# Attention value products in four groups per pair: units 6 and 7 joined to unit 8, behind the next pair's first score unit

## The chip, the cores and the metric

The kernel runs on one core of a Trainium2 chip. The metric is the device time of one launch in microseconds; of several runs the median counts. TensorE (PE in the rows) multiplies, ScalarE (ACT) takes exponentials and copies, VectorE (DVE) takes maxima and other elementwise work, GpSimd (POOL) does small elementwise work, SyncE (SP) issues most of the transfers.

## The reference, cut to what matters

The block is a half-weighted attention-and-experts layer, a sparse attention with selected keys, and the first layer once more with the same weights:

```
x = x + 0.5 * ffn_ref(layernorm(x), ...)
x = x + attn_ref(layernorm(x), ...)
x = x + 0.5 * ffn_ref(layernorm(x), ...)
```

The change lies in the attention inside `ffn_ref` (2 batches of 1024 tokens, 16 heads of width 8, causal):

```
scores = jnp.einsum('bhqd,bhkd->bhqk', q, k) / jnp.sqrt(jnp.float32(hd))
causal = jnp.tril(jnp.ones((s, s), bool))
scores = jnp.where(causal, scores, jnp.finfo(scores.dtype).min)
attn = jax.nn.softmax(scores, axis=-1)
o = jnp.einsum('bhqk,bhkd->bhqd', attn, v)
```

## The kernel before

The program is `pe_ffn`, `pe_sel`, `pe_ffn` on TensorE and the like on the others: two passes over the layer (c = 0 and 1) with the sparse attention between them. In each pass the heads go in 16 pairs (2 batches x 16 heads / 2), so there are 32 pairs in the whole program; the two heads of a pair lie side by side in the array.

For each pair three things are computed. The first pass over the scores (`PASS1`, `pe_pass1`, line 758, with a causal mask added at line 763) serves only to find each row's maximum, which VectorE takes (`dve_max`, lines 1431 and 1441). The second pass (`PASS2`, `pe_scores`, line 789) computes the scores transposed, with the maximum already subtracted, because rows with the maximum (the "maxrows") are loaded into the query tile by two transfers (line 485). ScalarE takes the exponential (line 1185) into one of six buffers `PT`. The value products (`pe_values`, line 811) multiply these by the values and sum into PSUM bank 6. Both passes are cut into 9 units (0 to 8) of 4 blocks of 128 x 128 for both heads. Units 1, 2, 4, 6 and 8 hold blocks on the diagonal; GpSimd cuts those to a triangle (`pool_cut`, line 699) after the exponential and before the value product: one cut or two.

`pe_step` works on three pairs at once and sets TensorE's order by hand. It begins at unit 5 (`HALFWAY`) of pair it and ends at unit 4 of pair it+1; at each unit TensorE does the score unit of the pair, then a first-pass unit of pair it+2 (`pe_next`), then, at some units, a value group. The value groups of a pair are `GROUPS = [(0, 1), (2, 3), (4, 5), (6, 7), (8,)]`; group 0 is done behind unit 4, group 1 behind unit 5, group 2 behind unit 7, group 3 behind unit 8, and group 4 behind unit 0 of the next pair. `pe_outputs` (line 821) turns the summed result behind unit 2 of the next pair. The last two pairs of a pass have no `pe_next`, and for the last one `pe_values` of groups 3 and 4 follow each other.

The waits that tie these together:

- A score unit waits for the maximum of the first-pass unit two places before it, whose PSUM pair it takes over, and unit 0 waits for both maxrow transfers as well (`maxrow_loaded`, line 779). `pe_next` waits for the exponential of the score unit one place before it.
- A value group waits for the last exponential in it, or, if its last unit is on the diagonal, for the cuts up to it (`cut_done`, line 805). Group 3 ends in unit 7, so it waits for exponential 7 and for cut 6; group 4 waits for cut 8.
- The maxrows of the next pair are turned by TensorE behind unit 6 (`pe_maxrows`, line 772), copied by ScalarE (line 1194), and sent by SyncE (line 485, two transfers).
- ScalarE's exponentials of the next pair wait for the value groups that free their buffer: unit 0 for group 1, unit 1 for group 2, and units 3 and 4 for group 3. Behind exponential 1 ScalarE waits for all groups of the pair and copies bank 6 away (line 1208), then goes on with exponential 2.
- SyncE loads the rows of pair it+4 when all groups of pair it are done (line 465).

In the names of the rows, `twin` is PSUM, `arena` holds the exponentials, maxima and values, `ffn` the query and key tiles.

Of the kernel before, what the change touches and what calls it, by code (L numbers as in the profile page):

```python
# [143 lines left out]
PASS2 = [[(0, 0)], [(1, 0)], [(0, 1)], [(1, 1), (1, 6)], [(1, 2), (1, 7)], [(0, 2), (0, 5)], [(0, 3), (0, 6)], [(1, 3), (1, 4)],  # L144
         [(0, 4), (1, 5)]]
UNITS = len(PASS1)
GROUPS = [(0, 1), (2, 3), (4, 5), (6, 7), (8,)]
GROUP_OF = [g for u in range(UNITS) for g, us in enumerate(GROUPS) if u in us]
EARLY = 4
HALFWAY = 5  # L150
# [10 lines left out]
def places(u):  # L161

    at, out = 0, []
    for g, kc in PASS2[u]:
        p = first_block(g, kc)
        out.append((g, kc, p, at))
        at += 4 - p
    assert at == 4
    return out
# [65 lines left out]
def build(nc, ins, const_ap, rot_ap, mask_ap, out):  # L235
# [10 lines left out]
    with ExitStack() as ctx:  # L246
# [207 lines left out]

        EXP0, PV0, ATT0, GELU0, Y0, ACC0, MAX0, OTURN0, OT0 = S_RING, len(GROUPS), 2, 4, 2, 2, S_RING, 1, 1
        block = ctx.enter_context(nc.Block())
# [4 lines left out]
        def sp_rows(sp, c, it, buf):  # L461

            g = PAIRS * c
            if not isinstance(it, int) or c:
                sp.wait_ge(pv_done, PV0 + len(GROUPS) * (g + it - RING + 1))
            pair = slice(it, it + 1) if isinstance(it, int) else bass.ds(it, 1)
# [300 lines left out]
        def pe_maxrows(pe, c, it):  # L767

            n = PAIRS * c + it
            pe.wait_ge(att_done, ATT0 + n - 1)  # L770
            pe.wait_ge(mb_ready, n + 1)
            pe.transpose(bank[7][:, :].bitcast(BF16)[:, 0:P], MB, ident_b[:, :]).then_inc(mt_done, 1)

        def pe_scores(pe, c, it, buf, u, left):

            n = PAIRS * c + it
            m = UNITS * it + u
            if u == 0:
                pe.wait_ge(maxrow_loaded, 32 * n + 32)
            if left >= 2:  # L780
                pe.wait_ge(max_done, MAX0 + TOTAL * c + m + UNITS + EARLY - 1)
            else:
                pe.wait_ge(max_done, MAX0 + TOTAL * c + min(m + UNITS + EARLY - 1, TOTAL))
                pe.wait_ge(exp_done, EXP0 + TOTAL * c + m - S_RING + 1)
            slot = 2 * u % S_RING
            for j, (g, kc, p, at) in enumerate(places(u)):
                for s in range(2):
                    r = slice(TILE * s, TILE * (s + 1))
                    x = pe.matmul(bank[2 * slot + s][:, at * P:(at + 4 - p) * P], KB[buf][r, kc * P:(kc + 1) * P],  # L789
                                  QB[buf][r, (4 * g + p) * P:(4 * g + 4) * P], start=(j == 0), stop=True, skip_group_check=True)  # L790
            x.then_inc(st_done, 1)

        def pe_next(pe, c, it, buf, m, u, visit):

            pe.wait_ge(exp_done, EXP0 + TOTAL * c + m)
            pe_pass1(pe, c, it, buf, u, visit, (2 * ((u + HALFWAY) % UNITS) + 1) % S_RING)

        def pe_values(pe, c, it, buf, group):

            n = PAIRS * c + it  # L800
            if group == 0:
                pe.wait_ge(ot_ready, OT0 + n)
            if GROUPS[group][-1] not in CUT:
                pe.wait_ge(exp_done, EXP0 + UNITS * n + GROUPS[group][-1] + 1)
            pe.wait_ge(cut_done, len(CUT) * n + len([u for u in CUT if u <= GROUPS[group][-1]]))
            for u in GROUPS[group]:
                for g, kc, p, at in places(u):
                    for s in range(2):
                        r = (2 * s + g) * STRIP
                        v = (s * TB + kc) * VW  # L810
                        m = pe.matmul(bank[6][r:r + STRIP, p * P:], VS[buf][:, v:v + STRIP],  # L811
                                      PT[(UNITS * buf + u) % PT_RING][:, s, at * P:(at + 4 - p) * P], start=(kc == 0), stop=True,
                                      skip_group_check=True)
            m.then_inc(pv_done, 1)

        def pe_outputs(pe, c, it):

            pe.wait_ge(att_done, ATT0 + PAIRS * c + it)
            pe.wait_ge(ot_ready, OT0 + PAIRS * c + it + 1)
            for t in range(4):  # L820
                m = pe.transpose(bank[7][:, t * P:(t + 1) * P], OT[:, t * P:(t + 1) * P], ident)
            m.then_inc(o_turned, 1)

        def pe_step(pe, c, b, it, buf, left, visit):
            two, one = (buf + 2) % RING, (buf + 1) % RING
            for u in range(HALFWAY, UNITS):
                pe_scores(pe, c, it, buf, u, left)
                if left >= 2:
                    pe_next(pe, c, it + 2, two, UNITS * it + u, u - HALFWAY, visit + (buf + 2) // RING)
                if u == HALFWAY:  # L830
                    pe_values(pe, c, it, buf, 1)
                if u == HALFWAY + 1 and left >= 1:
                    pe_maxrows(pe, c, it + 1)
                if u == HALFWAY + 2:
                    pe_values(pe, c, it, buf, 2)
                if u == HALFWAY + 3:
                    pe_values(pe, c, it, buf, 3)
            if left == 0:
                pe_values(pe, c, it, buf, 4)
                pe_outputs(pe, c, it)  # L840
                return
            for u in range(HALFWAY):
                pe_scores(pe, c, it + 1, one, u, left)
                if left >= 2:
                    pe_next(pe, c, it + 2, two, UNITS * (it + 1) + u, u + EARLY, visit + (buf + 2) // RING)
                if u == 0:
                    pe_values(pe, c, it, buf, 4)
                if u == 2:
                    pe_outputs(pe, c, it)
                if u == 4:  # L850
                    pe_values(pe, c, it + 1, one, 0)

        def pe_ffn(pe, c):
# [29 lines left out]
            for u in range(HALFWAY):  # L883
                pe_scores(pe, c, 0, 0, u, PAIRS)
                pe_next(pe, c, 1, 1, u, u + EARLY, 0)
            pe_values(pe, c, 0, 0, 0)
            run_steps(pe, pe_step, c)

            pe.wait_ge(att_done, ATT0 + PAIRS * (c + 1))
# [1043 lines left out]
```

## Time and profile before

| | us |
|---|---|
| median of 3 runs | 1869.47 (1865.15, 1869.47, 1881.36) |
| the profiled execution | 1864.45 |
| its span, first to last instruction | 1862.3 |

| engine | busy us | share of the span |
|---|---|---|
| TensorE matmul | 1476.3 | 79% |
| VectorE | 1244.6 | 67% |
| ScalarE | 996.6 | 54% |
| GpSimd | 445.8 | 24% |

The pairs run from about 78 to 304 us (first pass over the layer) and from about 1384 to 1609 us (second). Shares of the whole span say little about them: the experts and the sparse attention take the rest. A timeline of one pair, read row by row, shows what each engine waits for; a row with a bracket gives the idle time ahead of an instruction and what ended it. Rows of the same line that follow each other are merged, so the start of the next line's row tells when an engine went on.

### The profile page before, as it was taken

The numbers are of one execution on the slowest core, as the hardware profiler recorded it, in microseconds if no ns is written. First come the engines' busy times: TensorE is split into PE (matmuls) and PEld (weight loads), VectorE is DVE, ScalarE is ACT, GpSimd is POOL, SyncE is SP. The second block draws the span as 40 slices with busy tenths as digits, with TensorE's granted clock in tenths as the row PEclk, the third lists the DMA queues.
The fourth block names the chain that finished last, engine by engine and source line by source line (L and its number), as shares of the span: only waits on it lengthen the run. The fifth ranks groups of instructions, "written<-read, shape, count | busy, mean of one in ns | idle before, by whom it ended". The sixth has DMA issues, their size and how long they took to land.

```text
span 1862.3 us, 31801 instructions
## 1 busy us (share of the span) xinstructions
PE 1476.3 (79%) x10514; PEld 948.3 (51%) x10580; DVE 1244.6 (67%) x2571; ACT 996.6 (54%) x1800; POOL 445.8 (24%) x751
## 2 busy tenths in 40 slices
PE   3699997899958365888877888778469999779995
PEld 2355554577744122455545555556335455467774
DVE  3688885577785657675666676644367788567777
ACT  2266665588846342434444445334226666568884
POOL 4122222000011500434344344440412232200000
PEclk8699998699987556988778899788769999879998
DMA  5111110121102234111121111120221110011110
GB/s 156 67 49 44 43 30 2 58 68 68 57 23 76 67 82 95 52 26 55 27 72 54 34 51 53 35 62 17 91 83 48 46 45 30 2 58 68 68 57 23
DMA packets 63685, 99.68 MB, mean 54 GB/s; under 512 B 20011, under 2 KB 43507, under 8 KB 61494
## 3 DMA queue, kind: packets, MB, share of 16 engines
q1 hardware_dynamic: 53910, 80.42, 14.0%
q0 software_dynamic: 8192, 16.79, 3.5%
q8 instruction: 72, 1.18, 0.3%
q10 hardware_dynamic: 1456, 0.84, 0.2%
q14 instruction: 55, 0.45, 0.1%
HBM read 73.42 MB, written 10.69 MB: 45 GB/s over the span
## 4 chain that ended last, share of the span: by engine, by line
PE 51%; DVE 11%; ACT 9%; issue 9%; another core or an unknown queue 6%; DMA 5%; DVEq 4%; SPq 2%; ACTq 1%; POOL 0%; POOLq 0%
PE twin L964 9%; PE twin L954 6%; PE twin L811 5%; PE twin L789 5%; PE twin L758 4%; PE twin L1118 4%; DMA ffn<-arena 3%; DVEq L1750 3%; ACT arena L1185 3%; ACT experts L1260 2%; PE twin L763 2%; PE twin L1146 1%; PE twin L1134 1%; PE twin L1162 1%
## 5 line engine op out<-in xcount | busy, mean ns | idle before, releaser
L1185 ACT ACTIVATE arena<-twin 128x1024 f32<-128x1024 f32 x288 | 293.9, 1024 | 176.5 <-PE twin L789 176.3
L736 POOL DMA_INDIRECT arena<-kv_rows,IDX x256 | 249.1, 973 | 447.4 <-PE twin L1165 308.6
L1441 DVE TENSOR_REDUCE arena<-twin 128x8 f32<-128x1024 f32 (+1 forms) x160 | 195.4, 1225 | 81.3 <-PE twin L758 41.9
L1490 DVE TENSOR_TENSOR experts<-arena,experts 128x512 fp32r<-128x512 f32 x256 | 171.6, 690 | 71.2 <-ACT experts L1260 71.2
L1258 ACT ACTIVATE arena<-twin,bias 128x512 f32<-128x512 f32 x256 | 185.8, 726 | 45.8 <-PE twin L954 45.8
L954 PE MATMUL twin<-experts,experts 128*128 128x512 f32 x768 | 196.7, 403 | 7.5 <-ACT experts L1260 5.5
L758 PE MATMUL twin<-ffn,ffn 64*128 64x128 f32 (+3 forms) x1152 | 154.1, 350 | 48.1 <-DMA arena<-arena 27.0
L1431 DVE TENSOR_REDUCE arena<-twin 128x2 f32<-128x1024 f32 x128 | 153.2, 1222 | 52.5 <-PE twin L758 49.0
L1260 ACT ACTIVATE experts<-twin,bias 128x512 fp32r<-128x512 f32 x256 | 187.1, 731 | 0.0
L964 PE MATMUL twin<-experts,experts 128*128 128x512 f32 x768 | 182.2, 389 | 0.0
L1814 DVE TENSOR_TENSOR HN<-twin,RT 96x512 f32<-96x512 f32 x128 | 87.3, 683 | 135.1 <-remote 85.1
L699 POOL TENSOR_SCALAR_AFFINE_SELECT arena<-arena 128x256 f32<-128x256 f32 x256 | 100.1, 409 | 316.2 <-ACT arena L1185 316.2
L954 PEld LDWEIGHTS twin<-experts,experts 128*128 128x128 f32 x768 | 143.8, 192 | 54.7 <-ACT experts L1260 22.2
L789 PE MATMUL twin<-ffn,ffn 64*128 64x128 f32 (+3 forms) x960 | 145.9, 368 | 25.0 <-DMA ffn<-arena 21.0
L811 PE MATMUL twin<-arena 128*32 128x128 f32 (+3 forms) x1920 | 159.7, 433 | 2.6 <-POOL arena L699 1.6
L964 PEld LDWEIGHTS twin<-experts,experts 128*128 128x128 f32 x768 | 144.2, 188 | 30.4
L633 POOL TENSOR_TENSOR rstd<-vareps,neghalf 128x8 f32<-128x8 f32 x14 | 23.5, 1676 | 549.0 <-DVE vareps L1420 549.0
L758 PEld LDWEIGHTS twin<-ffn,ffn 64*128 64x128 f32 x1152 | 96.6, 202 | 78.6 <-ACT arena L1185 30.9
L789 PEld LDWEIGHTS twin<-ffn,ffn 64*128 64x128 f32 x960 | 76.6, 188 | 115.4 <-issue 75.1
L1392 ACT ACTIVATE ATT<-twin,col 128x256 f32<-128x256 f32 x128 | 60.7, 474 | 133.7 <-DVE col L1823 103.1
L1385 ACT ACTIVATE ATT<-twin 128x384 f32<-128x384 f32 (+1 forms) x128 | 55.8, 436 | 122.1 <-remote 112.7
L1118 PE MATMUL twin<-XN,arena 128*128 128x512 bf16 x374 | 113.2, 447 | 8.5 <-issue 7.4
(253 smaller groups left out, 2291.2 us busy)
## 6 DMA issues: line engine op xcount, KB each, us to landing
arena<-wt_rows SPq DMA_DIRECT2D x16, 1024.0 KB, 4.9
arena<-in_L_ffn_w SPq DMA_DIRECT2D x32, 256.0 KB, 5.2
ffn<-q_rows SPq DMA_DIRECT2D x64, 128.0 KB
ffn<-k_rows SPq DMA_DIRECT2D x64, 128.0 KB
XT<-idx_rows SPq DMA_DIRECT2D x16, 512.0 KB
q_rows<-ffn SPq DMA_DIRECT2D x8, 512.0 KB, 4.9
k_rows<-ffn SPq DMA_DIRECT2D x4, 1024.0 KB, 9.2
arena<-kv_rows,IDX POOLq DMA_INDIRECT x256
```

Of the source, the lines that this page charges most:

```text
L736: pool.indirect_dma_start(G[d % GR][:, g, :], None, kv_rows, bass.IndirectOffsetOnAxis(ap=IDX[:, q, k * GB + g:k * GB + g + 1], axis=0))\
L758: m = pe.matmul(bank[2 * slot + s][:, at * P:(at + blocks) * P], QB[buf][r, q * P:(q + 1) * P], KB[buf][r, k0 * P:(k0 + blocks) * P], star ...
L789: x = pe.matmul(bank[2 * slot + s][:, at * P:(at + 4 - p) * P], KB[buf][r, kc * P:(kc + 1) * P], QB[buf][r, (4 * g + p) * P:(4 * g + 4) * ...
L811: m = pe.matmul(bank[6][r:r + STRIP, p * P:], VS[buf][:, v:v + STRIP], PT[(UNITS * buf + u) % PT_RING][:, s, at * P:(at + 4 - p) * P], sta ...
L954: m = pe.matmul(bank[f][:, :], W1R[buf][w][:, f * P:(f + 1) * P], XR[x][:, tb * BANK:(tb + 1) * BANK], start=((w, x) == pairs[0]), stop=(( ...
L964: m = pe.matmul(bank[4 + k][:, :], W2R[buf][w][:, f, :], H1R[k][x][:, f, :], start=(f == 0 and (w, x) == pairs[0]), stop=(f == FC - 1 and ...
L1118: m = pe.matmul(o[:, :], TAB[part][:, 4 * b + c, :], OH[OH_AT[x][c] % OHR][:, :], start=(c == 0 and part == 0), stop=(c == n - 1 and part ...
L1185: act.activation(PT[(UNITS * buf + u) % PT_RING].rearrange("p s n -> p (s n)"), twin[2 * u % S_RING][:, :], ACT.Exp, scale=float(HD) ** -0 ...
L1258: act.activation(H1[tb % 2][:, f, :], bank[f][:, :], ACT.Gelu_apprx_tanh, bias=bias1[buf][:, f:f + 1])
L1260: act.activation(H1R[tb % 2][0][:, f, :], bank[f][:, :], ACT.Gelu_apprx_tanh, bias=bias1[buf][:, f:f + 1]).then_inc(gelu_done, 1)
L1441: dve.tensor_reduce(to, scores.rearrange("p (s t k) -> p s t k", s=2, t=to.shape[2]), AX_X, ALU.max).then_inc(max_done, 1)
L1490: dve.tensor_tensor(H1R[tb % 2][1][:, f, :], H1[tb % 2][:, f, :], H1R[tb % 2][0][:, f, :].bitcast(F32), ALU.subtract)\
```

## The change

Units 6, 7 and 8 become one group, number 3, done where group 4 was done: behind score unit 0 and the first-pass unit of the next pair. Nothing stands any more behind unit 8. For the last pair of a pass the group follows the last score unit. The counts in the waits follow from `GROUPS`.

```diff
-GROUPS = [(0, 1), (2, 3), (4, 5), (6, 7), (8,)]
+GROUPS = [(0, 1), (2, 3), (4, 5), (6, 7, 8)]
@@
                 if u == HALFWAY + 2:
                     pe_values(pe, c, it, buf, 2)
-                if u == HALFWAY + 3:
-                    pe_values(pe, c, it, buf, 3)
             if left == 0:
-                pe_values(pe, c, it, buf, 4)
+                pe_values(pe, c, it, buf, 3)
                 pe_outputs(pe, c, it)
                 return
             for u in range(HALFWAY):
@@
                 if u == 0:
-                    pe_values(pe, c, it, buf, 4)
+                    pe_values(pe, c, it, buf, 3)
```

On TensorE, at the boundary between two pairs, the rows stand as follows before (program order; L789 is a score unit, L758 a first-pass unit, L811 a value group, L779 the wait for the maxrows; the first two rows are unit 8, the rows behind L779 are units 0 and 1 of the next pair):

```order
L789 MATMUL twin<-ffn_65,ffn_69 128x256 x4
L795 REGISTER_ALU
L758 MATMUL twin<-ffn_71,ffn_67 128x512 x2
L805 REGISTER_ALU
L811 MATMUL twin<-arena 32x384 x2
L811 MATMUL twin<-arena 32x128 x2
L811 MATMUL twin<-arena 32x256 x4
L779 ISA
L781 ISA
L789 MATMUL twin<-ffn_66,ffn_70 128x512 x2
```

Here the value products of units 6 and 7 (the three rows of L811) stand between the first-pass unit and the wait for the maxrows. The difference at this place and at the next value group, which was that of unit 8 alone:

```order
 L758 MATMUL twin<-ffn_71,ffn_67 128x512 x2
-L805 REGISTER_ALU
-L811 MATMUL twin<-arena 32x384 x2
-L811 MATMUL twin<-arena 32x128 x2
-L811 MATMUL twin<-arena 32x256 x4
 L779 ISA
 L781 ISA
```

```order
 L758 MATMUL twin<-ffn_71,ffn_67 128x384 x2
 L805 REGISTER_ALU
-L811 MATMUL twin<-arena 32x256 x4
+L811 MATMUL twin<-arena 32x384 x2
+L811 MATMUL twin<-arena 32x128 x2
+L811 MATMUL twin<-arena 32x256 x8
 L781 REGISTER_ALU
 L789 MATMUL twin<-ffn_66,ffn_70 128x512 x2
```

The eight matmuls of units 6 and 7 left the first place, and the second has twelve where it had four; the last row, score unit 1 of the next pair, now has all twelve in front of it. Each matmul of the order is two in the trace (float32), so 16 left and 24 stand where 8 stood.

## Rows read from the trace of the kernel before

**Rows 1.** Chain of waits from 186 us: start, length, what held it
```profile
186.68 0.27 ACT arena L1194
186.95 0.02 issue
186.96 0.82 SPq L485
187.79 0.04 issue
187.83 2.20 DMA ffn<-arena
190.03 0.12 issue
190.15 0.50 PE twin L789 x2
190.65 0.29 PE twin L758 x4
190.94 0.58 PE twin L811 x8
```

**Rows 2.** Timeline of one boundary, all engines: start, length, engine, line, [idle, releaser]
```profile
159.22 0.40 PE L758 MATMUL twin<-ffn,ffn 64*128 64x512 f32 x2
159.50 1.02 ACT L1185 ACTIVATE arena<-twin 128x1024 f32<-128x1024 f32 x1 [1.06 <-PE twin L789]
159.55 1.08 PE L811 MATMUL twin<-arena 128*32 128x384 f32 x16
160.66 0.77 POOL L699 TENSOR_SCALAR_AFFINE_SELECT arena<-arena 128x256 f32<-128x256 f32 x2 [2.36 <-ACT arena L1185]
160.70 0.50 PE L789 MATMUL twin<-ffn,ffn 64*128 64x512 f32 x2
161.03 0.45 PE L758 MATMUL twin<-ffn,ffn 64*128 64x128 f32 x4
161.48 0.64 PE L811 MATMUL twin<-arena 128*32 128x256 f32 x8
162.05 0.50 PE L789 MATMUL twin<-ffn,ffn 64*128 64x512 f32 x2
162.67 1.02 ACT L1185 ACTIVATE arena<-twin 128x1024 f32<-128x1024 f32 x1 [0.41 <-PE twin L789]
163.75 0.50 PE L758 MATMUL twin<-ffn,ffn 64*128 64x256 f32 x4 [0.44 <-ACT arena L1185]
```

**Rows 3.** The same timeline, TensorE, value groups 0, 1 and 2 and what follows each
```profile
153.03 1.06 PE L811 MATMUL twin<-arena 128*32 128x512 f32 x8
154.02 0.50 PE L789 MATMUL twin<-ffn,ffn 64*128 64x384 f32 x4
...
154.74 1.07 PE L811 MATMUL twin<-arena 128*32 128x512 f32 x12
155.74 0.50 PE L789 MATMUL twin<-ffn,ffn 64*128 64x384 f32 x4
...
157.86 1.08 PE L811 MATMUL twin<-arena 128*32 128x384 f32 x16
158.88 0.51 PE L789 MATMUL twin<-ffn,ffn 64*128 64x256 f32 x4
```

**Rows 4.** Timeline, boundary 14 of the first pass and the last pair's end
```profile
291.50 0.49 PE L789 MATMUL twin<-ffn,ffn 64*128 64x512 f32 x2 [0.45 <-DMA ffn<-arena]
...
294.82 0.63 PE L821 MATMUL twin<-const,arena 128*128 128x128 f32 x4 [1.47 <-ACT arena L1208]
...
302.88 0.64 PE L811 MATMUL twin<-arena 128*32 128x256 f32 x8 [0.65 <-POOL arena L699]
```

**Rows 5.** Stretches of the pairs: busy us (instructions) by engine, granted clock, DMA
```profile
90.00:207.00 117.00, 109.05 (x1072) 59.35 (x1080) 93.16 (x112) 76.67 (x89) 33.93 (x104) 1.00 0.14 45
280.00:310.00 30.00, 24.12 (x248) 14.76 (x250) 9.70 (x23) 19.82 (x25) 7.36 (x21) 1.00 0.01 3
```

**Rows 6.** Timeline, ScalarE's copy of bank 6 in two pairs in a row
```profile
148.91 0.59 ACT L1208 ACTIVATE arena<-twin 128x512 f32<-128x512 f32 x1
...
163.59 0.59 ACT L1208 ACTIVATE arena<-twin 128x512 f32<-128x512 f32 x1
```

## The prediction

> **What bounds the kernel now.** First I read the pairs' granted clock and busy shares, since a mean over the program hides them: from 90 to 207 us TensorE is busy 109.05 of 117 us, VectorE 93.16, ScalarE 76.67, at a granted clock of 1.00 [rows 5]. So TensorE's order sets the pair's length, and at the upper of its two clock levels. That alone does not say that every matmul lies on the path. The chain of waits says where it does not: it leaves TensorE at the copy of the maxrows on ScalarE (186.68), goes through SyncE's issue (186.96) and the transfer (187.83, 2.20 us), and comes back to TensorE with score unit 0 of the next pair at 190.15 [rows 1]. In that stretch of 3.2 us TensorE does score unit 8, a first-pass unit and value groups, and none of it is in the chain.
>
> Next I read one boundary row by row [rows 2]. Behind unit 8 the first-pass unit starts at 159.22, the value group of units 6 and 7 at 159.55, score unit 0 of the next pair at 160.70, its first-pass unit at 161.03, the value group of unit 8 at 161.48, score unit 1 at 162.05. On the other engines exponential 8 runs from 159.50 to 160.52 and its two cuts on GpSimd from 160.66 to 161.43. Score unit 1 releases exponential 1 (162.67, one step of 1.02), and that releases the first-pass unit at 163.75, ahead of which TensorE is idle for 0.44 us.
>
> **The change part by part.** *What leaves the old place.* Sixteen matmuls of the trace, the group at 159.55. Groups of the same size with nothing to wait for behind them take, from their start to the start of what follows, 154.02 - 153.03 = 0.99, 155.74 - 154.74 = 1.00 and 158.88 - 157.86 = 1.02 us [rows 3]. This one takes 160.70 - 159.55 = 1.15 [rows 2], so score unit 0 waited 0.13 us more than the group explains, and the chain shows for what: the maxrow transfers. When the group is gone, TensorE is free at about 159.6, but score unit 0 still cannot start before the transfers have landed, about 3.2 us after their issue [rows 1], an issue that the change does not touch. So it stays at 160.70, and I credit the removal with nothing; TensorE idles about 1.1 us there.
>
> There is a second lid on any gain. Suppose the transfers were early: unit 0 could start at about 159.6, but its first-pass unit waits for exponential 8 (160.52), and the joined group waits for the cuts of unit 8, over at 161.43. Score unit 8, which leads to these, lies ahead of both places and does not move. So the joined group starts at 161.48 as before, whatever unit 0 does.
>
> *What comes to the new place.* The group at 161.48 takes 162.05 - 161.48 = 0.57 us for the columns of one unit spread over both halves of the output strips; the full groups have twice the columns per strip and take 1.00 on average. Twice as many columns thus cost 0.43 us more, and the joined group has three times those of unit 8: 0.57 + 2 x 0.43 = 1.43 us. The order of its units in the strips differs a little from those of rows 3, and no group of three is in the trace. Bounds: at best 0.57 + 2 x (0.99 - 0.57) = 1.41, with one entry and one exit for the group; at worst the sum of both groups as they are, 1.02 + 0.57 = 1.59. That is a growth of 0.84 to 1.02, and I take 0.86, since the step between group sizes is measured and the entry is saved.
>
> *Where the delay goes.* Score unit 1 starts 0.86 later, and everything that follows hangs on it. Queued behind the group on TensorE are score unit 1, first-pass unit 5, score unit 2. Exponential 1 waits for score unit 1 and slips by as much, then the first-pass unit at 163.75. The 0.44 us of idle there are no reserve: they are the time of exponential 1, counted from score unit 1, and remain. ScalarE's copy of bank 6 stands behind exponential 1 (which in rows 2 ends at 163.69, 1.64 us behind the end of the group), so its wait for all groups adds nothing more. Exponentials 3 and 4, which need the old group 3, come behind that copy already. SyncE's row loads start 0.86 later, but so do their readers, more than a pair ahead. VectorE gets its maxima later and has slack: 23.84 us of 117 [rows 5]. From unit 2 on to the turning of the maxrows the chain stays on TensorE's queue, so the next transfers, and with them the next unit 0, slip by the full amount.
>
> *The low clock.* The idle at the boundary grows from about 0.13 to 1.1 us. In this trace a boundary with idles of 0.45 and 1.47 us [rows 4] lies in a stretch with a granted clock of 1.00 [rows 5], which is the 2.4 GHz level. So I keep the clock. The Trainium skill, "TensorE: Matmul & The Clock Gate", section "A second HAM failure mode: psum-queue depth-cycling", says that short idles between groups of matmuls can make the clock swing between its two levels; by it this change would cost more than the moved matmuls, and it is a rival below. The rows with more idle speak against it here.
>
> *How many times.* The 14 boundaries of each pass that still have first-pass work are as in rows 2. Boundary 14 waits for the transfer too, with 0.45 us idle [rows 4], so its group is covered as well. Behind the last pair's unit 8 the old group of units 6 and 7 ran while GpSimd cut unit 8; after it TensorE waited another 0.65 us until 302.88 for those cuts [rows 4]. Now all three units start at 302.88: again 0.86. That is 16 per pass, 32 in all.
>
> **Sum.** 32 x 0.86 = 27.5 us, bounds 32 x 0.84 = 26.9 and 32 x 1.02 = 32.6. Against the profiled execution's 1864.45 that is 1892; the median of the three runs is 5 us above it, which makes 1897. I say 1895, or 1.4% slower. The copies of bank 6 of two pairs in a row start 163.59 - 148.91 = 14.68 us apart [rows 6]; that should grow to about 15.55 us.
>
> **The rivals.**
>
> *The delay is absorbed (no change).* This is the case on the other side. It needs a wait on TensorE between score unit 1 and the turning of the maxrows that score unit 1 does not itself cause, such as VectorE freeing a PSUM pair late. It decides in favour of no change if such a wait is 0.86 us or more in each pair; half of it gives 1864 + 14 = 1878 to 1883. The busy 109.05 of 117 leave 8 us over 8 pairs, 1.0 per pair, and 0.44 of that is exponential 1, so at most 0.5 could be there. With all of it absorbed the kernel would stay at 1869.
>
> *The saved switch counts (slightly faster).* If score unit 0 were not held by the transfers and the joined group not by the cuts, only one entry to a group would be saved: 1.02 + 0.57 - 1.43 = 0.16 us, 32 times, 5 us: 1864. Both holds would have to be misread.
>
> *The joined group is longer than its columns.* At 1.59 us or somewhat more, because units 6 and 7 follow each other in the same strips: 33 us or more, 1902.
>
> *The clock falls.* If one tenth of TensorE's work in the pairs ran at 1.2 GHz, that is at double length, a pair would grow by another 109.05 / 8 x 0.1 = 1.4 us, 32 times 44 us: about 1939.
>
> **How the numbers follow.** My forecast has 0.74; the longer group 0.09; the fallen clock 0.04; partly or fully absorbed 0.11; the saved switch 0.02. The range 1880 to 1910 takes in the forecast against either base, the longer group and half absorption, and leaves out the clock and full absorption. One per cent, about what a measurement of this kernel can tell from no change, is 18.7 us, so the limit lies at 1888: the forecast is beyond it save for a scatter like that of the runs (1865 to 1881). Slower 0.84, within 1% 0.14, faster 0.02.
>
> **What would show it.** In the profile after: score unit 0 (L789) still about 3.1 to 3.2 us behind the issue at L485, now with some 1.1 us of idle ahead of it, released by the transfer; the L811 group behind it with 24 matmuls, starting as the cuts of L699 end; score unit 1 about 1.43 us behind the group's start where it was 0.57; the copies at L1208 about 15.55 us apart; a granted clock of 1.00 from 90 to 280 us; nothing changed in the length of the experts and the sparse attention. I would be wrong if unit 0 and the group both started earlier against L1194, if the group took about 1.0 us, or if the copies stayed 14.7 us apart.

## The result, and the profile after

The changed kernel takes 1898.49 us (median of 4 runs, 1893.88 to 1904.39) where the kernel before takes 1867.31 (4 runs, 1861.28 to 1881.36). The ratio is 1.0159, with a 95% interval of 1.0125 to 1.0192: slower by about 30 us. The profiled execution has a span of 1891.7 us, 29.4 more than the span before.

Where those 29.4 us lie can be read from stretches of the two traces that end at the same event, ScalarE's copy of bank 6 in the first and in the last pair of each pass. Columns: stretch, its length, busy us (instructions) of TensorE, its weight loads, VectorE, ScalarE, GpSimd, then granted clock, share and GB/s of the transfers. The kernel before:

```profile
0.00:90.11 90.11, 46.37 (x264) 28.37 (x266) 44.57 (x94) 23.36 (x44) 26.18 (x53) 0.73 0.38 112
90.11:303.59 213.48, 196.94 (x1948) 106.57 (x1962) 158.37 (x195) 142.59 (x164) 62.48 (x190) 1.00 0.12 38
303.59:1395.40 1091.81, 825.64 (x5446) 540.51 (x5482) 695.96 (x1659) 515.58 (x1140) 287.88 (x314) 0.81 0.19 56
1395.40:1608.43 213.03, 197.12 (x1948) 106.61 (x1962) 158.24 (x195) 142.51 (x164) 62.49 (x190) 1.00 0.12 38
1608.43:1862.30 253.87, 210.19 (x908) 166.24 (x908) 187.45 (x430) 172.52 (x292) 6.72 (x4) 0.89 0.15 50
```

The changed kernel:

```profile
0.00:90.58 90.58, 47.16 (x266) 28.69 (x266) 44.58 (x94) 23.36 (x44) 26.18 (x53) 0.76 0.38 112
90.58:318.46 227.88, 195.30 (x1962) 107.46 (x1962) 158.35 (x195) 142.60 (x164) 62.48 (x190) 0.99 0.12 35
318.46:1412.04 1093.58, 836.19 (x5482) 540.72 (x5482) 694.93 (x1659) 515.01 (x1141) 287.51 (x314) 0.82 0.19 55
1412.04:1639.45 227.41, 195.03 (x1962) 107.48 (x1962) 158.24 (x195) 142.53 (x163) 62.47 (x190) 0.99 0.11 35
1639.45:1891.70 252.25, 208.55 (x908) 164.59 (x908) 187.47 (x430) 172.14 (x292) 6.72 (x4) 0.90 0.15 51
```

The two stretches of pairs grow by 14.40 and 14.38 us; the others change by +0.47, +1.77 and -1.62. TensorE's busy time in the pairs does not grow (196.94 to 195.30 us): the added time is idle. The two traces have 1948 and 1962 matmul records there, so the small fall is not read.

One boundary in the timeline of the changed kernel, which answers to [rows 2] (start, length, engine, line, idle ahead and its releaser):

```profile
177.14 1.62 SPq L485 DMA_DIRECT2D ffn<-arena  x2
...
178.80 0.39 PE L758 MATMUL twin<-ffn,ffn 64*128 64x512 f32 x2
179.08 1.02 ACT L1183 ACTIVATE arena<-twin 128x1024 f32<-128x1024 f32 x1 [1.06 <-PE twin L789]
...
180.23 0.77 POOL L699 TENSOR_SCALAR_AFFINE_SELECT arena<-arena 128x256 f32<-128x256 f32 x2 [2.37 <-ACT arena L1183]
...
180.33 0.50 PE L789 MATMUL twin<-ffn,ffn 64*128 64x512 f32 x2 [1.14 <-DMA ffn<-arena]
...
180.66 0.46 PE L758 MATMUL twin<-ffn,ffn 64*128 64x128 f32 x4
...
181.06 1.52 PE L811 MATMUL twin<-arena 128*32 128x384 f32 x24
...
182.51 0.49 PE L789 MATMUL twin<-ffn,ffn 64*128 64x512 f32 x2
```

Score unit 0 starts 3.19 us behind the issue at L485, as in [rows 1] (186.96 to 190.15), with 1.14 us of idle ahead of it that the transfer ends. The cuts of unit 8 are over at 181.00 and the joined group of 24 matmuls starts at 181.06. Score unit 1 follows 1.45 us behind the group's start; before it was 0.57. The chain of waits passes here, as in [rows 1], through the transfer and then the group:

```profile
161.28 0.27 ACT arena L1192
...
161.56 0.83 SPq L485
...
162.44 2.17 DMA ffn<-arena
...
164.72 0.50 PE twin L789 x2
...
165.51 1.49 PE twin L811 x20
```

The copies of bank 6 (now line 1206) start 15.58 us apart in the first seven intervals of the first pass, where they were 14.70. Two of them in a row:

```profile
168.46 0.59 ACT L1206 ACTIVATE arena<-twin 128x512 f32<-128x512 f32 x1
...
184.04 0.59 ACT L1206 ACTIVATE arena<-twin 128x512 f32<-128x512 f32 x1
```

The last interval, which belongs to the pair without first-pass work, grows from 9.51 to 11.62 us. That is more than 0.88, and the experiments below take it up.

### The profile page after: what moved, and what is told of

Read it like the earlier page. It is cut to its first block, busy times and chain, and to the rows that moved or that the text cites. A ratio compares the mean times of both kernels' runs of the same rounds, so it can differ in the third digit from the quotient of the medians.

```text
span 1891.7 us, 31827 instructions
## 1 busy us (share of the span) xinstructions
PE 1482.2 (78%) x10580; PEld 948.9 (50%) x10580; DVE 1243.6 (66%) x2571; ACT 995.6 (53%) x1800; POOL 445.4 (24%) x751
## 4 chain that ended last, share of the span: by engine, by line
PE 50%; DVE 12%; ACT 9%; issue 8%; another core or an unknown queue 7%; DMA 6%; DVEq 4%; SPq 3%; ACTq 1%; POOL 0%; POOLq 0%
PE twin L962 9%; PE twin L952 6%; PE twin L811 6%; PE twin L789 5%; PE twin L758 4%; DMA ffn<-arena 4%; PE twin L1116 3%; DVEq L1748 3%; ACT arena L1183 2%; PE twin L763 2%; ACT experts L1258 2%; PE twin L1144 1%; SPq L485 1%; DVE best L1789 1%
## 5 line engine op out<-in xcount | busy, mean ns | idle before, releaser
L758 PE MATMUL twin<-ffn,ffn 64*128 64x128 f32 (+3 forms) x1152 | 152.1, 346 | 54.5 <-DMA arena<-arena 26.5
L789 PE MATMUL twin<-ffn,ffn 64*128 64x128 f32 (+3 forms) x960 | 142.8, 361 | 54.8 <-DMA ffn<-arena 52.5
L811 PE MATMUL twin<-arena 128*32 128x128 f32 (+3 forms) x1920 | 155.6, 438 | 4.8 <-POOL arena L699 4.5
L789 PEld LDWEIGHTS twin<-ffn,ffn 64*128 64x128 f32 x960 | 76.6, 188 | 140.8 <-issue 80.2
L758 PEld LDWEIGHTS twin<-ffn,ffn 64*128 64x128 f32 x1152 | 98.5, 202 | 85.1 <-ACT arena L1183 39.6
L1116 PE MATMUL twin<-XN,arena 128*128 128x512 bf16 x408 | 129.8, 469 | 0.2 <-DVE HN L1812 0.2
```

What stands on the lines that cost most here:

```text
L758: m = pe.matmul(bank[2 * slot + s][:, at * P:(at + blocks) * P], QB[buf][r, q * P:(q + 1) * P], KB[buf][r, k0 * P:(k0 + blocks) * P], star ...
L1116: m = pe.matmul(o[:, :], TAB[part][:, 4 * b + c, :], OH[OH_AT[x][c] % OHR][:, :], start=(c == 0 and part == 0), stop=(c == n - 1 and part ...
```

## The experiments

The theory has three parts: the products of units 6 and 7 were free where they stood, because TensorE waits there for the maxrow transfers; they could not start the group earlier in the new place, because the transfers and, behind them, the cuts of unit 8 hold it; and score unit 1, hence exponential 1, hence the pair, pays for the group's length. Rivals: the wait of the joined group for the cuts makes the loss, or the transfer alone, or the clock. The table sums up the two kernels and the nine experiments. Each ratio compares a kernel with the kernel before in the same series of runs, whose median was 1867.31 us for the changed kernel, 1869.40 for e2 to e5 and 1865.59 for e1 and e6 to e8. "Pair" is the mean of the first seven intervals between copies of bank 6 in the first pass, "last" its last interval, "first copy" the start of the first.

| kernel | ratio to before (95%) | first copy | pair us | last us |
|---|---|---|---|---|
| before | 1 | 90.11 | 14.70 | 9.51 |
| changed | 1.0159 (1.0125 to 1.0192) | 90.58 | 15.58 | 11.62 |
| e2 without products 6 and 7 | 1.0014 (0.9989 to 1.0039) | 91.52 | 14.70 | 11.95 |
| e1 moved, not joined | 1.0136 (1.0095 to 1.0176) | 90.27 | 15.54 | 9.50 |
| e3 no transfer to wait for | 1.0073 (1.0047 to 1.0099) | 83.08 | 15.57 | 10.74 |
| e4 no cuts of unit 8 | 1.0117 (1.0073 to 1.0161) | 91.84 | 15.54 | 9.45 |
| e5 neither | 0.9952 (0.9932 to 0.9972) | 82.94 | 15.15 | 9.47 |
| e6 last pair split | 1.0153 (1.0112 to 1.0193) | 91.21 | 15.58 | 9.51 |
| e9 last pair's idle filled | one run | 90.95 | 15.57 | 10.36 |
| e7 unit 8 behind score unit 1 | 0.9951 (0.9927 to 0.9974) | 89.26 | 14.23 | 9.52 |
| e8 joined group behind score unit 1 | 1.0017 (0.9999 to 1.0036) | 88.27 | 14.81 | 10.57 |

### e2: were the products free in the old place?

```diff
             for u in GROUPS[group]:
+                if u in (6, 7):
+                    continue
                 for g, kc, p, at in places(u):
```

(on the changed kernel)

> The changed kernel with the value products of units 6 and 7 left out (so its attention sums lack them); the group behind the next pair's first score unit is unit 8 alone, as before the change. My theory: in the kernel before, these products ran while TensorE had to wait for the maxrow transfers anyway, so taking them out of it altogether gives nothing: 1862 to 1869 us, copies at L1206 14.6 to 14.7 us apart, score unit 0 still 3.1 to 3.2 us behind the issue at L485 with 1.0 to 1.2 us idle ahead of it. Rival (the products were on the path): 32 x 1.0 us less than before, about 1835 us, copies 13.7 us apart.

The ratio to the kernel before is 1.0014 (0.9989 to 1.0039), the pair 14.70 us, the same as before. Leaving out 16 matmuls of a pair buys nothing. TensorE's timeline shows the hole that they filled, released by the transfer, and the small group at 0.57 us as before:

```profile
176.89 0.49 PE L789 MATMUL twin<-ffn,ffn 64*128 64x512 f32 x2 [1.13 <-DMA ffn<-arena]
177.22 0.45 PE L758 MATMUL twin<-ffn,ffn 64*128 64x128 f32 x4
177.61 0.64 PE L813 MATMUL twin<-arena 128*32 128x256 f32 x8
178.18 0.50 PE L789 MATMUL twin<-ffn,ffn 64*128 64x512 f32 x2
```

The changed kernel differs from this one only by those products, in their new place, and costs 0.88 us a pair more. So the old place was free and the new one is not. The median, 1872.39 us, is 3 us over the upper end that I gave; the kernel before had 1869.4 beside it. The last interval is 11.95, 2.4 more than before (11.93 in the second pass). The rows say why:

```profile
295.00:301.00 6.00, 4.88 (x27) 2.47 (x28) 0.64 (x4) 3.83 (x5) 1.58 (x4) 0.50 0.00 0
...
306.62 0.64 PE L813 MATMUL twin<-arena 128*32 128x256 f32 x8 [2.11 <-POOL arena L699]
```

From 295 to 301 us, behind the boundary into the last pair, the granted clock was at its lower level, 0.50, and TensorE's work of that stretch took longer. Ahead of the very last group stand 2.11 us of idle, and that group ran at its usual 0.64 us. So the 2.4 us were lost ahead of that idle and not in it.

### e1: the move or the join?

```diff
-                if u == HALFWAY + 3:
-                    pe_values(pe, c, it, buf, 3)
             if left == 0:
+                pe_values(pe, c, it, buf, 3)
                 pe_values(pe, c, it, buf, 4)
@@
                 if u == 0:
+                    pe_values(pe, c, it, buf, 3)
                     pe_values(pe, c, it, buf, 4)
```

(on the kernel before)

> The kernel before with its five groups; only the place of group 3 (units 6 and 7) moves, to just ahead of group 4 (unit 8) behind the next pair's first score unit and first-pass unit. The last pair keeps the old order. My theory: score unit 1 slips by a whole group of 1.0 us in 30 pairs, pairs of 15.6 to 15.75 us, 1896 to 1901 us: the move alone makes the loss, and joining saves about 0.15 us per pair of it. Rival (the loss comes from the joined group's wait for the cuts of unit 8): units 6 and 7 need no such wait here, so pairs of 14.7 to 15.1 us and 1867 to 1880 us.

The ratio is 1.0136 (1892.08 us, below the 1896 to 1901 that I gave) and the pair 15.54 us. The rival falls: units 6 and 7 wait for no cut of unit 8 here, and the loss is still there. But my own number was off too. TensorE's timeline:

```profile
180.23 0.45 PE L758 MATMUL twin<-ffn,ffn 64*128 64x128 f32 x4
180.61 1.52 PE L811 MATMUL twin<-arena 128*32 128x384 f32 x24
182.06 0.50 PE L789 MATMUL twin<-ffn,ffn 64*128 64x512 f32 x2
```

The two separate groups take 182.06 - 180.61 = 1.45 us together, what the joined one takes too. In length, two groups that stand next to each other are no longer than one of the same columns; the join itself saves nothing, and the sum of the two lengths, 1.59, which I had as the upper bound, is not reached. The pair is 0.04 us shorter than in the changed kernel.

### e3, e4, e5: what holds the joined group?

e3 sends the maxrows to memory that nothing reads and drops the wait; e4 leaves unit 8 out of the cuts; e5 does both.

```diff
-                sp.dma_start(QB[buf][r:r + MAXROWS, :].bitcast(F32).rearrange("r (t q) -> r t q", q=P),
+                sp.dma_start(HNf[s * MAXROWS:(s + 1) * MAXROWS, 0:L].rearrange("r (t q) -> r t q", q=P),
@@
-            if u == 0:
-                pe.wait_ge(maxrow_loaded, 32 * n + 32)
@@
             pe.wait_ge(att_done, ATT0 + PAIRS * (c + 1))
+            pe.wait_ge(maxrow_loaded, 32 * PAIRS * (c + 1))
```

(e3; the last line makes TensorE wait for the transfers once, when all pairs of a pass are done)

```diff
-CUT = [u for u in range(UNITS) if diagonals(u)]
+CUT = [u for u in range(UNITS) if diagonals(u) and u != 8]
```

(e4)

> The changed kernel, but the maxrows are sent to memory nobody reads and score unit 0 does not wait for them (the maxima are not subtracted before the exponential). My theory of two lids: score unit 0 starts about 1.1 us earlier, its first-pass unit about 0.45 us earlier (behind exponential 8), but the joined group still starts when the cuts of unit 8 are over, so the time stays within 3 us of the changed kernel, about 1895 to 1900 us. Rival (the transfer alone holds the boundary): 28 x 1.1 us less, about 1868 us.

The pair is 15.57 us against 15.58: for the pairs the theory of two lids holds to 0.01 us. The timeline of e3 shows score unit 0 right behind the first-pass unit (171.51), the next first-pass unit waiting for exponential 8, and the group waiting for the cuts:

```profile
171.28 0.39 PE L758 MATMUL twin<-ffn,ffn 64*128 64x512 f32 x2
171.51 0.40 PE L787 MATMUL twin<-ffn,ffn 64*128 64x512 f32 x2
172.64 0.55 PE L758 MATMUL twin<-ffn,ffn 64*128 64x128 f32 x4 [0.73 <-ACT arena L1182]
173.54 1.52 PE L809 MATMUL twin<-arena 128*32 128x384 f32 x24 [0.34 <-POOL arena L699]
```

Score unit 0 is early and nothing comes of it. The total nevertheless fell, to a ratio of 1.0073 (1881.05 us), which is outside what I had written. The table says where: the first copy of the pass comes at 83.08 instead of 90.58, because the very first pair also stops waiting for its transfer. First the changed kernel, then e3:

```profile
69.00 0.80 PE L789 MATMUL twin<-ffn,ffn 64*128 64x512 f32 x2 [9.49 <-DMA ffn<-arena]
```

```profile
60.89 0.80 PE L787 MATMUL twin<-ffn,ffn 64*128 64x512 f32 x2 [1.25 <-DVE arena L1428]
```

The second pass has the same (9.78 us of idle against 1.25). The last interval is 10.74 instead of 11.62, and not through the missing wait: the idle ahead of the last group is 2.11 us in both kernels, but in e3 the granted clock fell only while the group ran, and it took 1.90 us instead of 2.79. That is 7.5 + 0.9 = 8.4 us a pass, 17 in all, about the 17.4 by which the medians differ (16 by the ratios). I had priced the boundaries and forgotten that the edit also takes the wait off the start.

> The changed kernel without the triangle cuts of unit 8 on GpSimd (its diagonal blocks stay uncut); the joined group waits for exponential 8 instead. My theory: the maxrow transfer still sets score unit 0 and with it the group's start, so the pairs stay at 15.5 to 15.6 us; only the last pair of each pass gains, 0.8 us by itself, up to 2 if its clock stays up: 1894 to 1898 us. Rival (the cuts alone hold the group): 28 x 0.45 or more, 1885 us or less.

The pair stays at 15.54, the last interval falls to 9.45, the median is 1893.8 us, just below what I gave: as the theory has it, the cuts alone hold nothing in the pairs. In the last pair the group then waits for exponential 8 alone. One thing was not foreseen: the interval before the last, with the boundary into the pair without first-pass work, is 15.95 us here against 14.86 in the changed kernel, and TensorE's timeline shows why:

```profile
303.56 0.50 PE L789 MATMUL twin<-ffn,ffn 64*128 64x512 f32 x2 [1.54 <-DMA ffn<-arena]
303.99 2.58 PE L811 MATMUL twin<-arena 128*32 128x384 f32 x24
```

The group takes 2.58 us instead of 1.52: in this execution the granted clock had fallen here (0.50 from 305 to 307 us), and in the second pass too (15.90 against 14.65).

> Both of the last two together: maxrows sent aside and unit 8 not cut. My theory: with both lids off the group starts behind the first-pass unit that waits for exponential 8, about 0.45 us earlier than in the changed kernel, 28 times, and the two ends of a pass gain too: pairs of about 15.1 us, 1880 to 1886 us. The joined group still costs its length behind exponential 8, so the time does not come back to 1867. Rival (any idle ahead of unit 0 is given back once nothing holds it): pairs of 14.5 us, 1866 us.

The pair is 15.15 us, 0.43 less than in the changed kernel, against 0.45 expected. With both lids off the group starts earlier, at 0.49 us behind its first-pass unit's start, which waits for exponential 8:

```profile
170.37 0.55 PE L758 MATMUL twin<-ffn,ffn 64*128 64x128 f32 x4 [0.73 <-ACT arena L1182]
170.86 1.52 PE L809 MATMUL twin<-arena 128*32 128x384 f32 x24
```

The rival's pair of 14.5 us is out. The median, 1860.31, is far below my 1880 to 1886, for the reason of e3 (7.6 us a pass at the start) and 2.15 us a pass in the last interval (0.9 because the group starts earlier, the rest because it runs at the upper clock). Those, the pairs (13 x 0.43) and boundary 14 (1.1) add up to 33 us; the ratios of the two kernels differ by 0.0207, 39 us, and the spans of the two profiled executions by 26.3 us, because in this one the part between the two passes' pairs took some 7 us longer. e5's profiled run was the slowest of its ten. The sum is thus right only to some 6 us either way, about the width of the intervals, and what the remainder is stays open.

### e6 and e9: why the last pair costs 2.1 us

The tail of the changed kernel, TensorE's timeline:

```profile
313.01 0.50 PE L789 MATMUL twin<-ffn,ffn 64*128 64x256 f32 x4
315.63 2.79 PE L811 MATMUL twin<-arena 128*32 128x384 f32 x24 [2.11 <-POOL arena L699]
```

Here the same 24 matmuls take 2.79 us instead of 1.52. In the stretches of that trace the granted clock is 1.00 until 313 and 0.50 from 316 to 319:

```profile
306.00:313.00 7.00, 5.54 (x62) 2.89 (x60) 0.64 (x4) 6.38 (x8) 1.61 (x5) 1.00 0.00 0
313.00:316.00 3.00, 0.89 (x12) 0.50 (x12) 0.00 (x0) 1.68 (x2) 1.51 (x4) 0.95 0.02 5
316.00:319.00 3.00, 2.42 (x24) 1.18 (x16) 0.00 (x0) 0.54 (x1) 0.00 (x0) 0.50 0.00 0
```

Before, the products of units 6 and 7 lay in this idle (the row of 302.88 in [rows 4] has 0.65 ahead of it). e6 gives them back their place in the last pair only:

```diff
+            if split:
+                pe.wait_ge(exp_done, EXP0 + UNITS * n + 8)
+                pe.wait_ge(cut_done, len(CUT) * n + 4)
...
-            pe.wait_ge(cut_done, len(CUT) * n + len([u for u in CUT if u <= GROUPS[group][-1]]))
+            if not split:
+                pe.wait_ge(cut_done, len(CUT) * n + len([u for u in CUT if u <= GROUPS[group][-1]]))
             for u in GROUPS[group]:
+                if split and u == 8:
+                    pe.wait_ge(cut_done, len(CUT) * n + 5)
```

> The changed kernel, but in the last pair of each pass the products of units 6 and 7 do not wait for the cuts of unit 8; those of unit 8 do. My theory: the profile after shows the last joined group at 2.79 us behind 2.11 us of idle, because the clock fell to its lower level in the idle; without that idle the group runs at the upper level again, and the last two copies at L1206 lie 9.5 us apart instead of 11.6: 4 us less than the changed kernel. Rival (only the order matters, not the clock): 0.9 us per pass, 1.8 in all.

The last interval is 9.51 us, as before the change. The total, 1.0153, can't tell 4 us from 2, the less so as in the second pass of the profiled execution the clock fell one boundary earlier (that interval is 16.12 us against 14.65 in the changed kernel). And e6 takes away the idle and the order together. e9 therefore keeps the wait and the order of the changed kernel and only fills the idle:

```diff
             if left == 0:
+                pe.wait_ge(exp_done, EXP0 + UNITS * (PAIRS * c + it) + 7)
+                for _ in range(8):
+                    pe.matmul(bank[0][:, :], ident_b[:, :], mask_qk[:, :, :].rearrange("p a q -> p (a q)"),
+                              start=True, stop=True, skip_group_check=True)
                 pe_values(pe, c, it, buf, 3)
```

> The changed kernel with eight idle-filling matmuls (a constant times a constant, result not read) in the last pair of each pass, between the last score unit and the joined group, while TensorE waits there for the cuts of unit 8. The wait itself stays. Clock theory: the fall to the lower level in this idle is what stretches the last group; filled, it runs at a granted clock of 1.00, takes 1.45 to 1.55 us, and the last two copies at L1206 lie 10.3 to 10.5 us apart (9.51 and 0.88) instead of 11.62. Rival (the group is long for another reason, such as its wait for the cuts or its 24 matmuls after a wait): still 2.7 to 2.8 us and 11.6.

```profile
313.28 0.50 PE L789 MATMUL twin<-ffn,ffn 64*128 64x256 f32 x4
313.72 1.90 PE L839 MATMUL twin<-mask_qk_b,ident_b 128*128 128x512 bf16 x8
315.90 1.52 PE L811 MATMUL twin<-arena 128*32 128x384 f32 x24 [0.28 <-POOL arena L699]
```

The group starts at the same distance from the score unit (315.90 - 313.28 = 2.62 us, in the changed kernel 315.63 - 313.01 = 2.62), takes 1.52 us at a granted clock of 1.00, and the last interval is 10.36 us in both passes, 0.85 over the kernel before. So of the 2.11 us, 0.85 are the group's length on the path and 1.26 are the lower clock. That the group ran at the lower clock is read from the changed kernel's own rows. That the idle brings the fall rests on less: e9 is one run, on a chip where the kernel before took 1748.04 us and this one 1772.48, and the changed kernel without filler was not run there. Only its trace is used; its pairs are 15.57 us, as on the first chip.

Nor does such an idle always cost the same. Four kernels have the 2.11 us of idle ahead of the last group, each in both passes. In the changed kernel the clock fell before the group (2.79 and 2.81 us), in e3 and e8 while it ran (1.90, 1.77, 1.73 and 1.68 us), and in e2 the group kept its 0.64 us. At the boundary into the last pair seven kernels have 1.40 to 1.56 us of idle ahead of score unit 0: there the clock fell in six of fourteen cases (both passes of e2 and e4, the second of e6 and e8) and held in eight (both passes of the changed kernel, e1 and e9, the first of e6 and e8). With 1.56 us it fell in two cases and held in one. So the length of one idle does not decide it, and what does stays open.

### e7 and e8: the group behind score unit 1

If exponential 1 pays for what stands ahead of score unit 1, a group should stand behind it. e7 does this with unit 8 of the kernel before, e8 with the joined group. The edit of e7:

```diff
                 pe_scores(pe, c, it + 1, one, u, left)
+                if u == 1:
+                    pe_values(pe, c, it, buf, 4)
                 if left >= 2:
                     pe_next(pe, c, it + 2, two, UNITS * (it + 1) + u, u + EARLY, visit + (buf + 2) // RING)
-                if u == 0:
-                    pe_values(pe, c, it, buf, 4)
```

(on the kernel before; e8 is the same edit on the changed kernel, with group 3)

> The kernel before with group 4 (unit 8) moved from ahead of score unit 1 of the next pair to just behind it. Score unit 1 then starts 0.57 us earlier; exponential 1 follows exponential 0 without a gap and ends 0.35 to 0.4 us earlier, and the group fills idle of TensorE. My theory: 0.35 to 0.4 us per pair less, pairs of 14.3 us, 1855 to 1859 us. Rival (VectorE's maxima or exponential 0 take the place of the wait): no gain, 1865 to 1869 us.

The ratio is 0.9951 (0.9927 to 0.9974), 1855.65 us, and the pair 14.23, 0.47 us less than before. TensorE's timeline across the boundary has no idle that the trace reports:

```profile
172.27 0.50 PE L789 MATMUL twin<-ffn,ffn 64*128 64x512 f32 x2
172.60 0.47 PE L758 MATMUL twin<-ffn,ffn 64*128 64x128 f32 x4
172.89 0.40 PE L789 MATMUL twin<-ffn,ffn 64*128 64x512 f32 x2
173.22 0.64 PE L811 MATMUL twin<-arena 128*32 128x256 f32 x8
173.88 0.55 PE L758 MATMUL twin<-ffn,ffn 64*128 64x128 f32 x4
...
174.80 0.50 PE L758 MATMUL twin<-ffn,ffn 64*128 64x256 f32 x4
```

This version beats both kernels.

> The changed kernel with the joined group (units 6, 7 and 8) moved behind score unit 1 of the next pair, ahead of its first-pass unit. My theory: the group no longer delays exponential 1, but it delays the two matmul units behind it; of its 0.86 us growth about 0.45 to 0.6 fall into the idle that exponential 1 left: pairs of 14.9 to 15.0 us, 1874 to 1880 us. Rival (only the total of TensorE's work and idle counts, wherever the group stands): pairs of 15.5 us, 1895 us.

The pair is 14.81 us, 0.77 less than in the changed kernel and 0.11 more than before; the ratio is 1.0017 (0.9999 to 1.0036).

```profile
175.26 0.39 PE L789 MATMUL twin<-ffn,ffn 64*128 64x512 f32 x2
175.58 1.52 PE L811 MATMUL twin<-arena 128*32 128x384 f32 x24
```

The same 24 matmuls, with 1.16 us of idle ahead of unit 0 here and 1.14 in the changed kernel, make a pair 0.77 us shorter when they stand behind score unit 1. So the place matters, and the rival that counts only work and idle falls. But the 0.11 us over the kernel before are not the price of the joined group in the new place, since moving unit 8 alone gained 0.47 (e7). What units 6 and 7 cost there is the difference between e8 and e7: 14.81 - 14.23 = 0.58 us. Behind score unit 1 their products thus cost 0.58 us a pair, ahead of it 0.88, and in the old place nothing. I had expected 14.9 to 15.0 and undersized the gain.

## Why the prediction was right

Forecast: 1895 us, 1.4% slower, 1880 to 1910, and 27.5 us in the sum. Measured: 1898.49, 1.59% slower, 29.4 us between the profiled executions' spans. By its steps:

- *The removal gains nothing.* Right, for the reason given: e2 has the same pair length as the kernel before, and score unit 0 starts 3.19 us behind the issue with 1.14 us idle (about 1.1 was forecast).
- *A second lid.* Right in the pairs: e3 and e4 each leave the pair within 0.04 us, and e5 takes 0.43 off.
- *The group's length.* 0.57 + 0.86 = 1.43 was forecast, 1.45 measured, a growth of 0.88. The reasoning for the choice was half right. I credited the join with a saved entry and set 1.59 as the upper bound without it; e1 shows 1.45 without the join. So the step per column that I took from the other groups held in either form, and the saving that I put down to the join is not the join's. The rival of the longer group falls with that.
- *The whole delay goes through.* Right: the pair grows from 14.70 to 15.58 (15.55 was forecast). No wait on TensorE absorbs any of it. The case of absorption is out.
- *The clock.* Right for the pairs, where [rows 5] has 1.00; in the changed kernel the stretches of pairs have 0.99 with the two tails in them, and the first pass has 1.00 from 90 to 310 us and from 306 to 313. The swing of which the Trainium skill warns in "TensorE: Matmul & The Clock Gate", section "A second HAM failure mode: psum-queue depth-cycling", did not appear at the boundaries between the pairs with first-pass work. The step failed for the last pair: there I took the group for one more 0.86 and did not count that the idle ahead of it grows to 2.11 us. It cost 2.11 us, of which e9 assigns 1.26 to the clock. At the boundary ahead of it I kept the clock because a boundary with 0.45 and 1.47 us of idle had 1.00 [rows 4]; with the change the 0.45 became 1.41 and 1.56 in the two passes. The clock held there in the changed kernel's profiled execution and fell in those of e2, e4, e6 and e8, so that this part came right was in part luck.
- *The sum.* 15 intervals of the first pass: 14 grow by 216.26 - 203.97 = 12.29 in all (0.88 each) and the last by 2.11, together 14.40; the second pass has 14.38. With the first boundary, which lies ahead of the first copy, this is 30.5 us, where the sum had 27.5; 2.5 of the difference is the clock in the two last pairs, 0.5 the growth of 0.88 instead of 0.86. The rest of the program gave 1 us back. On the measured base of 1867.31 the sum gives 1894.8, and the median is 3.7 us above that, about what was left out here.

## What to carry to other kernels

An idle engine is not a reserve everywhere: the same value products cost nothing ahead of a score unit that waits for a transfer, 0.88 us a pair ahead of the score unit that feeds the next exponential, and 0.58 behind it. Moving the small group of unit 8, too, to the place behind that score unit made the kernel before faster by 0.47 us a pair. Before work is moved, ask of each place which wait ends last there and what is the first thing queued behind it that another engine waits for. And when an edit takes a wait away, price the start and the end of the loop too: there the same wait was worth 7.5 us once a pass, against nothing in each pair. And before an experiment's gain is put down to a place, compare it with the kernel that differs in that one thing only: e8 against e7, not against the kernel before.

## What the runs showed of the hardware that was not expected

Two value groups of different units that stand next to each other take as long as one joined group of 24 matmuls, 1.45 us in e1 and in the changed kernel, though in e1 a wait that is already met stands between them.

In the changed kernel the clock fell to its lower level, 1.2 GHz, in the last pair of both passes, behind 2.11 us of reported idle; TensorE had been busy for 5.54 of the 7 us up to 313. The same 24 matmuls took 2.79 instead of 1.52 us; with 1.90 us of filler matmuls in that idle, in one run on another chip, it stayed at 2.4 GHz. The fall does not follow from the length of that idle alone: behind the same 2.11 us the group of e3 took 1.90 us and that of e2 its usual 0.64, and with 1.40 to 1.56 us of idle one boundary earlier the clock fell in six of fourteen cases. Idles of 1.14 us between busy stretches, one in each of the pairs with first-pass work, did not lower it.
